# A decoder layer with a mixture of experts: the last layer norm moved into the last two experts

## The chip, the cores and the metric

One NeuronCore of one Trainium2 chip runs the kernel. The metric is device microseconds (us) of one execution; 1935.22 us is the median of three runs of the kernel before.

## The reference, cut to what matters

The last part of the layer, on N = 4096 tokens (rows) of D = 512 values, with 32 experts and 8 experts per token:

```
x      = layernorm(layernorm(x + self_attention) + cross_attention)
logits = x @ gate.T;  topw, topi = top_k(softmax(logits), 8);  topw /= topw.sum()
for each expert e: h = silu(rows_e @ gate_e) * (rows_e @ up_e);  out_e = h @ down_e
ffn    = sum over a token's 8 experts of topw * out_e
out    = layernorm(x + ffn)
```

An expert holds up to 512 rows (CAP). A slot that no token fills points at one of 512 spare rows behind the 4096.

## The kernel before, in words

The layer norms, the attentions and the routing come first (batches of 256 tokens, software-pipelined by hand-written lists of steps) and are not touched. After them `acc_rows` in HBM, 4096 + 512 rows of fp32, holds the input of the expert layer, and each expert adds its rows into it.

**The expert loop.** Experts 0 to 31 (NX = 32) run one after another, with two sets of buffers, k = 0 for even and k = 1 for odd ones. Each engine has its own instruction queue in program order, and semaphores tie them together:

- TensorE: `up_gate` (L1127 on): three column blocks f, for each the gate and the up matmuls (24 matmuls of 128x512 a block, fp32 emulated by three fp16 products, all recorded at L679). Then `down` (L1145): 36 matmuls into four banks `ps_y[c]`, f outermost. The last expert has `down_last` (L1161) in place of it: it waits for all of h and goes c outermost, so that `ps_y[0]` is ready first.
- ScalarE: splits the high part of the next expert's weights (L1289), takes the silu of each gate block (L1545), then writes `y[:, k, c] = ps_y[c] * cur_w` (L1554), four ACTIVATEs of 128x512.
- VectorE: splits the low part of the next expert's weights (L1579), and for each f makes h in three instructions (L2211 product, L2216 cast, L2218 remainder).
- GpSimd: copies the expert's routing weights (L2471), gathers the rows of expert e + 2 by four indirect DMAs of 128 rows (L2477), waits until all scatters of the expert before have landed (`st_y`), copies the row numbers (`column_out`, L2464) and scatters y with four indirect DMAs that add in memory (`scatter`, L2490, `compute_op=ALU.add`).
- SyncE (SP): loads the weights of expert e + 2 into `stage[:, place]`, waits for the gathered rows and transposes them (`turn_tokens`, L629) for TensorE.

**The last stage.** SP waits for `st_y` = 32 * 64, that is until every scatter has landed (L657). It then loads `acc_rows` in 8 groups of 512 rows (GROUPS = 8, GT = 4 tiles of 128 rows, 1 MB each, L666) into `rows3`, which lies over the weights' arena. For each group VectorE makes four `bn_stats` (L2235), four `bn_aggr` (L2238) and two small instructions (L2240, L2241); GpSimd raises the variance to the power -1/2 and makes the shift (L2527, L2529); ScalarE scales four tiles in place (L1569); SP stores the group to `out` (L669) and waits at the end for all eight stores.

Rows are laid out `(t p)`, so each partition's four rows of a group lie apart in HBM and one contiguous piece has 2 KB:

```python
            def group_rows(ap, g):
                return ap[bass.ds(g * GT * P, GT * P), :].rearrange("(t p) n -> p t n", p=P)
```

## Time and profile before

| | us |
|---|---|
| median of 3 runs | 1935.22 (1933.79 to 1937.46) |
| the profiled execution, its own time | 1940.54 |
| its span, first to last record | 1938.7 |
| TensorE busy | 1818.9 (94% of the span) |
| VectorE, ScalarE, GpSimd busy | 1163.9, 978.0, 1218.6 |
| from the last matmul's end to the end of the span | 52.7 (from 1886.0) |

All times of day in this document are microseconds from the start of the span. TensorE's time fills the span up to 1886.0, where the last expert's matmuls end; behind them stand the last scatters, the loads, the norm and the stores.

### The profile page before, as it was taken

The page shows a single profiled execution, that of the slowest core. Times are in us where ns is not written, and L with a number is a line of the kernel's source. Part 1 is how long each engine was busy: PE and PEld are TensorE (multiplying, and loading weights), DVE is VectorE, ACT ScalarE, POOL GpSimd, SP SyncE. Part 2 cuts the span into 40 slices and gives each one's busy share as a digit, 9 for nine tenths or more (in the row PEclk, how much of TensorE's full clock was granted, in tenths as well). Part 3 has the DMA queues.
Part 4 walks back from the last instruction along what each step waited for, and adds up shares of the span by engine and source line. Part 5 has one row for each costly group of instructions (what it writes and reads, how often), then busy time and mean ns, then how long its engine had stood idle before and what let it go on. Part 6 is the DMA issues. An engine that isn't in the chain of part 4 may idle for free.

```text
span 1938.7 us, 43204 instructions
## 1 busy us (share of the span) xinstructions
PE 1818.9 (94%) x15510; PEld 1082.8 (56%) x15510; DVE 1163.9 (60%) x2145; ACT 978.0 (50%) x1969; POOL 1218.6 (63%) x992
## 2 busy tenths in 40 slices
PE   7999999999999999999996769999999999999980
PEld 4776676667767776777763424444444444444430
DVE  5546778777877787778776734444444444444434
ACT  6766666676666665766572313333333333333314
POOL 3766766776677767776775046666666656566632
PEclk8999999999999999999998779999999999999995
DMA  8775776566566656576647389999999999999949
GB/s 236 144 134 115 138 137 143 117 144 151 126 131 130 155 131 132 120 158 136 133 100 174 106 220 233 234 243 233 239 231 245 241 248 241 246 231 235 199 58 352
DMA packets 619374, 345.17 MB, mean 178 GB/s; under 512 B 519344, under 2 KB 541872, under 8 KB 619312
## 3 DMA queue, kind: packets, MB, share of 16 engines
q1 hardware_dynamic: 590368, 274.09, 59.1%
q0 software_dynamic: 28944, 70.27, 17.5%
q8 instruction: 36, 0.59, 0.1%
q14 instruction: 26, 0.21, 0.0%
HBM read 158.67 MB, written 60.29 MB: 113 GB/s over the span
## 4 chain that ended last, share of the span: by engine, by line
PE 88%; DMA 3%; ACT 3%; DVE 3%; issue 2%; POOL 1%; SPq 1%; ACTq 0%; DVEq 0%; POOLq 0%
PE bank L679 62%; PE bank L1145 12%; PE bank L745 5%; PE bank L717 5%; ACT arena_wo L1569 1%; PE bank L873 1%; PE bank L689 1%; PE bank L780 1%; DMA arena_a<-stage 1%; DMA arena_p<-x_rows,cur_from 0%; PE bank L817 0%; DVE s_max L1609 0%; DMA stage<-wkT 0%; ACT qk L1202 0%; DMA arena_wo<-acc_rows 0%
## 5 line engine op out<-in xcount | busy, mean ns | idle before, releaser
L679 PE MATMUL bank<-arena_x,arena_wo 128*128 128x256 f16 (+1 forms) x4224 | 611.3, 303 | 8.2 <-ACT qk L1202 5.3
L679 PEld LDWEIGHTS bank<-arena_x,arena_wo 128*128 128x128 f16 x4224 | 409.1, 98 | 196.8 <-issue 10.7
L2490 POOL DMA_INDIRECT acc_rows<-arena_wo,cur_to x128 | 274.5, 2144 | 240.7 <-ACT arena_wo L1554 211.2
L2273 POOL TENSOR_TENSOR arena_p<-arena_p 128x512 f16<-128x512 f32 x256 | 329.3, 1308 | 109.8 <-ACT arena_p L1221 109.8
L1579 DVE SCALAR_TENSOR_TENSOR arena_wo<-stage,arena_wo 128x3072 f16<-128x3072 f32 (+2 forms) x70 | 174.2, 2490 | 290.2 <-ACT arena_wo L1289 280.1
L679 PE MATMUL bank<-arena_v,arena_wo 128*128 128x512 f16 x1152 | 253.9, 382 | 18.0 <-DMA arena_v<-arena_p 18.0
L1145 PE MATMUL bank<-arena_wo 128*128 128x512 f16 x1116 | 245.9, 379 | 0.0
L2268 POOL TENSOR_TENSOR qk<-qk 128x512 f16<-128x512 f32 x128 | 161.6, 1263 | 116.7 <-ACT qk L1202 116.6
L1212 ACT ACTIVATE arena_p<-bank,s_neg 128x256 f32<-128x256 f32 x512 | 203.4, 504 | 15.9 <-DVE s_neg L1612 13.4
L1554 ACT ACTIVATE arena_wo<-bank,cur_w 128x512 f32<-128x512 f32 x128 | 79.8, 686 | 256.8 <-PE bank L1145 246.9
L1200 ACT ACTIVATE qk<-bank,bqkv 128x256 f32<-128x256 f32 x256 | 123.2, 481 | 153.3 <-PE bank L679 152.8
L679 PEld LDWEIGHTS bank<-arena_v,arena_wo 128*128 128x128 f16 x1152 | 113.2, 98 | 156.2 <-issue 22.0
L1545 ACT ACTIVATE arena_a<-bank 128x512 f32<-128x512 f32 x96 | 57.0, 594 | 271.8 <-PE bank L679 262.7
L1609 DVE TENSOR_REDUCE s_max<-bank 128x2 f32<-128x512 f32 x256 | 164.2, 683 | 40.6 <-PE bank L717 40.4
L1145 PEld LDWEIGHTS bank<-arena_wo 128*128 128x128 f16 x1116 | 109.2, 98 | 131.7
L679 PE MATMUL bank<-arena_wo,arena_x 128*128 128x512 f16 x768 | 178.2, 382 | 0.0
L1221 ACT ACTIVATE arena_p<-arena_p 128x512 f16<-128x512 f32 x256 | 152.1, 668 | 43.4 <-issue 39.8
L679 PE MATMUL bank<-arena_wo,arena_a 128*128 128x512 f16 x768 | 171.0, 379 | 1.1 <-DVE arena_r L1646 0.8
L2477 POOL DMA_INDIRECT arena_p<-x_rows,cur_from x124 | 129.5, 1044 | 53.3 <-issue 27.1
L2211 DVE SCALAR_TENSOR_TENSOR arena_a<-bank,arena_a 128x512 f32<-128x512 f32 x96 | 66.0, 688 | 139.7 <-PE bank L679 139.6
L1289 ACT ACTIVATE arena_wo<-stage 128x3072 f16<-128x3072 f32 (+1 forms) x62 | 131.2, 2118 | 0.5 <-DMA stage<-wdnT 0.5
L1202 ACT ACTIVATE qk<-bank,bqkv 128x256 f16<-128x256 f32 x256 | 123.7, 483 | 0.0
(183 smaller groups left out, 2310.1 us busy)
## 6 DMA issues: line engine op xcount, KB each, us to landing
stage<-wguT SPq DMA_DIRECT2D x31, 1536.0 KB
stage<-wdnT SPq DMA_DIRECT2D x31, 768.0 KB
arena_x<-xT SPq DMA_DIRECT2D x16, 512.0 KB, 4.2
arena_r<-x_rows SPq DMA_DIRECT2D x16, 512.0 KB, 5.2
stage<-ctxT SPq DMA_DIRECT2D x16, 512.0 KB, 4.4
x_rows<-arena_r SPq DMA_DIRECT2D x16, 512.0 KB, 3.0
acc_rows<-arena_r SPq DMA_DIRECT2D x16, 512.0 KB, 3.3
arena_wo<-acc_rows SPq DMA_DIRECT2D x8, 1024.0 KB, 10.8
```

The source lines that it names most:

```text
L679: mm = pe.matmul(out_ap, lhs(a, i), rhs(c, i), start=(n == 0 and i == 0), stop=(n == 2 and i == chunks - 1))
L1145: mm = pe.matmul(ps_y[c][:, :], hT[:, a, f, c * P:(c + 1) * P], ew_dn[:, k, w, f, :], start=(f == 0 and n == 0), stop=(f == FC - 1 and n = ...
L1202: ins = nc.scalar.activation(qk[:, j % 2, 0, at], ps_qk[:, at], ACT.Identity, bias=bqkv[:, w, j:j + 1], scale=1.0 / W_SCALE)
L1212: ins = nc.scalar.activation(probs[:, j % 2, h, t, :], ps_s[j % 2][h][:, t * S:(t + 1) * S], ACT.Exp, bias=s_neg[:, j % 2, n:n + 1], scale ...
L1221: nc.scalar.activation(halves[:, j % 2, h, 0, :], probs[:, j % 2, h].rearrange("p t k -> p (t k)"), ACT.Copy).then_inc(p_hi, 1)
L1289: nc.scalar.activation(ew[:, k, 0, part], stage[:, place, part], ACT.Copy, scale=W_SCALE).then_inc(ew_hi, 1)
L1579: return vec.scalar_tensor_tensor(out=dst, in0=src, scalar=scale, in1=hi, op0=ALU.mult, op1=ALU.subtract)
L1609: vec.tensor_reduce(s_max[:, j % 2, 2 * h:2 * h + 2], ps_s[j % 2][h][:, :].rearrange("p (t k) -> p t k", t=TT), AX.X, ALU.max).then_inc(s_ ...
L2268: gp.tensor_tensor(qk[:, j % 2, 1, :], qk32[:, j % 2, :], qk[:, j % 2, 0, :], ALU.subtract).then_inc(qk_lo, 1)
L2273: gp.tensor_tensor(halves[:, j % 2, h, 1, :], probs[:, j % 2, h].rearrange("p t k -> p (t k)"), halves[:, j % 2, h, 0, :], ALU.subtract).t ...
L2477: gp.indirect_dma_start(xg[:, k, c, :], None, x2_rows, bass.IndirectOffsetOnAxis(ap=cur_from[:, k, c:c + 1], axis=0)).then_inc(ld_xg[k], 16)
L2490: gp.indirect_dma_start(acc_rows, bass.IndirectOffsetOnAxis(ap=cur_to[:, k, c:c + 1], axis=0), y[:, k, c, :], None, compute_op=ALU.add).th ...
```

## The change

The last stage is started before the last two experts (30 and 31) have added their rows.

- Once the scatters of expert 29 have landed, SP loads the 8 groups of `acc_rows`, each into a buffer that is free by then: `stage`, `arena_r`, `arena_v` and the even weights' buffer. All eight are normalised and stored to `out`; for tokens of experts 30 and 31 these rows are still incomplete. The layout is now `(p t)`: a partition's four rows are neighbours in HBM, one piece of 8 KB.
- The rows of experts 30 and 31 are finished apart. GpSimd gathers their present sums (`gather_old`), VectorE adds `ps_y * cur_w` to them (`add_rows`, in place of ScalarE's L1554), writes the result to y, and normalises y as a ninth and tenth set (`late`, sets 6 and 9 in order). ScalarE's result goes back into the gathered buffer.
- Expert 30's sums are put back into `acc_rows` (`put_rows`, plain indirect writes) after all groups are loaded, since expert 31 may share tokens with it, and `gather_old` of expert 31 waits for that.
- When all eight stores have landed, the finished rows are written over them in `out` by row number, first expert 30's, and when those have landed expert 31's (`put_late`). `out` gets 512 spare rows, which the host cuts off.
- TensorE's `down_last` is gone; expert 31 uses `down`.
- The order in which the steps stand on VectorE, ScalarE, GpSimd and SP is written out by hand. On GpSimd `scales(0)` to `scales(4)` stand ahead of `put_rows`, `scales(5)` to `scales(9)` behind `gather_old` of expert 31; on VectorE both last groups stand ahead of `add_rows` of expert 31.
- The statistics' small buffers move to `x1T` and have 10 sets.

```diff
# SP
-            sp.wait_ge(st_y, NX * 64)
-            sp.wait_ge(y_done, NX * CC)
...
-            for g in range(GROUPS):
-                if g >= HALF:
-                    sp.wait_ge(ld_acc[g % HALF], 16)
-                sp.dma_start(rows3[:, g], group_rows(acc_rows, g)).then_inc(ld_acc[g % HALF], 16)
-            for g in range(GROUPS):
-                sp.wait_ge(out_done, (g + 1) * GT)
-                sp.dma_start(group_rows(out, g), rows3[:, g]).then_inc(st_out, 16)
+                return ap[bass.ds(g * GT * P, GT * P), :].rearrange("(p t) n -> p t n", p=P)
+            sp.wait_ge(st_y, (NX - LATE) * 64)
+            sp.wait_ge(ew_lo_gu, NX - 1)
+            sp.wait_ge(ew_lo_dn, NX - 1)
+            load_group(0)
+            load_group(1)
+            load_group(2)
+            sp.wait_ge(ew_lo_gu, NX)
+            sp.wait_ge(ew_lo_dn, NX)
+            load_group(3)
+            load_group(4)
+            sp.wait_ge(u_mm, (NX - 1) * FC)
+            load_group(5)
+            store_group(0)
+            sp.wait_ge(y_mm, (NX - 1) * CC)
+            load_group(6)
+            load_group(7)
+            for g in range(1, GROUPS):
+                store_group(g)
             sp.wait_ge(st_out, GROUPS * 16)
+            sp.wait_ge(st_late, LATE * 64)
# TensorE
-            up_gate(NX - 1, 1, NX // 2 * 64)
-            down_last(NX - 1, 1)
+            expert(NX - 1, 1, NX // 2 * 64)
# ScalarE
+            def scaled(n, dst, rows, done):
+                act.wait_ge(ln3_rstd, 2 * (n + 1))
+                for t in range(GT):
+                    nc.scalar.activation(dst[:, t, :], rows[:, t, :], ACT.Identity, bias=shift3[:, n, t:t + 1],
+                                         scale=rstd3[:, n, t:t + 1]).then_inc(done, 1)
...
+            gate_out(NX - 2, 0, 2)
+            group(0, 0)
+            gate_out(NX - 1, 1, 0)
+            group(1, 1)
+            gate_out(NX - 1, 1, 1)
+            group(2, 2)
+            gate_out(NX - 1, 1, 2)
+            group(3, 3)
+            group(4, 4)
+            group(5, 5)
+            late(6, 0)
+            group(7, 6)
+            group(8, 7)
+            late(9, 1)
# VectorE
+            def add_rows(e, k):
+                for c in range(CC):
+                    dve.wait_ge(y_mm, count(e, CC, c + 1))
+                    if c == 0:
+                        dve.wait_ge(cur_done, count(e, 2, 2))
+                        dve.wait_ge(ld_old[k], CC * 16)
+                    vec.scalar_tensor_tensor(out=y[:, k, c, :], in0=ps_y[c][:, :], scalar=cur_w[:, k, c:c + 1],
+                                             in1=old[k][:, c, :], op0=ALU.mult, op1=ALU.add).then_inc(y_done, 1)
...
+            up_out(NX - 2, 0, 2)
+            group(0, 0)
+            group(1, 1)
+            add_rows(NX - 2, 0)
+            group(2, 2)
+            up_out(NX - 1, 1, 0)
+            group(3, 3)
+            up_out(NX - 1, 1, 1)
+            group(4, 4)
+            up_out(NX - 1, 1, 2)
+            group(5, 5)
+            late(6, NX - 2, 0)
+            group(7, 6)
+            group(8, 7)
+            add_rows(NX - 1, 1)
+            late(9, NX - 1, 1)
# GpSimd
+            def put_rows(e, k):
+                for c in range(CC):
+                    wait_apart(pool, y_done, count(e, CC, c + 1), s_const, N_CONST)
+                    gp.indirect_dma_start(acc_rows, bass.IndirectOffsetOnAxis(ap=cur_to[:, k, c:c + 1], axis=0),
+                                          y[:, k, c, :], None).then_inc(st_y, 16)
...
+            pool.wait_ge(xg_turned[0], NX // 2 * 64)
+            weights_out(NX - 2, 0)
+            pool.wait_ge(cur_done, count(NX - 2, 2, 2))
+            pool.wait_ge(st_y, (NX - 2) * 64)
+            column_out(NX - 1, 1)
+            gather_old(NX - 2, 0)
+            pool.wait_ge(xg_turned[1], NX // 2 * 64)
+            weights_out(NX - 1, 1)
+            scales(0)
...
+            scales(4)
             for g in range(GROUPS):
+                pool.wait_ge(ld_acc[g], 16)
+            put_rows(NX - 2, 0)
+            pool.wait_ge(cur_done, count(NX - 1, 2, 2))
+            gather_old(NX - 1, 1)
+            for n in range(5, SETS):
+                scales(n)
+            pool.wait_ge(st_out, GROUPS * 16)
+            put_late(0, 0)
+            pool.wait_ge(st_late, CC * 16)
+            put_late(1, 1)
```

`up_out`, `gate_out`, `rows_out`, `spread`, `scales` are the old loops' bodies with names; `gather_old(e, k)` waits for `st_y >= e * 64` and issues four indirect reads of `acc_rows` into `old[k]`; `put_late(n, k)` issues four indirect writes from `old[k]` into `out`.

## Rows read from the trace of the kernel before

**Rows 1.** The profile's page: its first line, and the last chain's shares by engine.

```profile
span 1938.7 us, 43204 instructions
...
PE 88%; DMA 3%; ACT 3%; DVE 3%; issue 2%; POOL 1%; SPq 1%; ACTq 0%; DVEq 0%; POOLq 0%
```

**Rows 2.** The chain of work that ended last, in order of time: start, us, what.

```profile
1860.49 15.55 PE bank L679 x72
...
1880.23 0.70 ACT arena_wo L1554
...
1887.49 5.48 DMA acc_rows<-arena_wo,cur_to
...
1892.99 5.65 DMA arena_wo<-acc_rows
```

**Rows 3.** Timeline, GpSimd, expert 29's scatter, then the last expert's: start, us, engine, what.

```profile
1836.90 1.63 POOL L2490 DMA_INDIRECT acc_rows<-arena_wo,cur_to  x1 [5.53 <-ACT arena_wo L1554]
...
1840.72 4.67 POOL L2490 DMA_INDIRECT acc_rows<-arena_wo,cur_to  x1 [0.31 <-issue]
...
1850.70 0.19 POOL L2464 COPY cur_to<-idx_to 128x4 int32<-128x4 int32 x1 [3.13 <-DMA acc_rows<-arena_wo,cur_to]
...
1881.69 1.58 POOL L2490 DMA_INDIRECT acc_rows<-arena_wo,cur_to  x1 [14.00 <-ACT arena_wo L1554]
```

**Rows 4.** Timeline, the last loads and stores on SP's queue, and ScalarE's 32 scalings.

```profile
1892.99 14.56 SPq L666 DMA_DIRECT2D arena_wo<-acc_rows  x8
...
1903.13 23.37 ACT L1569 ACTIVATE arena_wo<-arena_wo,arena_r 128x512 f32<-128x512 f32 x32 [16.39 <-POOL arena_r L2529]
...
1907.59 20.22 SPq L669 DMA_DIRECT2D out<-arena_wo  x8
```

**Rows 5.** Busy time by stretch: PE, PEld, DVE, ACT, POOL, granted clock, DMA share, GB/s.

```profile
1855.00:1860.00 5.00, 5.00 (x25) 2.29 (x24) 0.00 (x0) 1.41 (x3) 0.00 (x0) 1.00 0.00 0
...
1865.00:1870.00 5.00, 5.00 (x25) 2.25 (x23) 1.81 (x3) 0.60 (x1) 2.39 (x3) 1.00 0.99 129
...
1928.00:1933.00 5.00, 0.00 (x0) 0.00 (x0) 0.00 (x0) 0.00 (x0) 0.00 (x0) 0.50 1.05 409
```

**Rows 6.** Timeline, VectorE's first two groups of the last stage and GpSimd's scales between.

```profile
1898.66 2.47 DVE L2235 BATCH_NORM_STATS2 arena_r<-arena_wo 128x6 f32<-128x512 f32 x4 [20.71 <-DMA arena_wo<-acc_rows]
...
1901.52 0.16 DVE L2241 TENSOR_SCALAR arena_r<-arena_r 128x4 f32<-128x4 f32 x1
1901.60 2.46 DVE L2235 BATCH_NORM_STATS2 arena_r<-arena_wo 128x6 f32<-128x512 f32 x4
...
1902.90 0.20 POOL L2529 TENSOR_TENSOR arena_r<-arena_r 128x4 f32<-128x4 f32 x1
```

**Rows 7.** Timeline, VectorE: h of expert 31's first block, and a weight split of expert 30.

```profile
1840.59 3.36 DVE L1579 SCALAR_TENSOR_TENSOR arena_wo<-stage,arena_wo 128x3072 f16<-128x3072 f32 x1 [9.26 <-ACT arena_wo L1289]
...
1865.71 0.69 DVE L2211 SCALAR_TENSOR_TENSOR arena_a<-bank,arena_a 128x512 f32<-128x512 f32 x1 [11.07 <-PE bank L679]
...
1866.97 0.69 DVE L2218 TENSOR_TENSOR arena_wo<-arena_a,arena_wo 128x512 f16<-128x512 f32 x1
```

**Rows 8.** Timeline, GpSimd: the last two gathers' issues, and SP's transposes that wait for them.

```profile
1828.66 0.96 POOL L2477 DMA_INDIRECT arena_p<-x_rows,cur_from  x1 [0.30 <-issue]
...
1829.92 0.96 POOL L2477 DMA_INDIRECT arena_p<-x_rows,cur_from  x1 [0.30 <-issue]
...
1833.80 5.36 SPq L629 DMA_TRANSPOSE arena_x<-arena_p  x4
```

**Rows 9.** Timeline, GpSimd: two scatter issues of expert 30, nothing beside them.

```profile
1863.77 1.56 POOL L2490 DMA_INDIRECT acc_rows<-arena_wo,cur_to  x1 [0.30 <-issue]
1865.64 1.56 POOL L2490 DMA_INDIRECT acc_rows<-arena_wo,cur_to  x1 [0.30 <-issue]
```

**Rows 10.** DMA issues: out<-in, queue, count, KB each, median us from issue to landing.

```profile
x_rows<-arena_r SPq DMA_DIRECT2D x16, 512.0 KB, 3.0
...
out<-arena_wo SPq DMA_DIRECT2D x8, 1024.0 KB, 12.9
```

169 lines of the change are left out of this document (99 added, 70 removed).

## The prediction

> **What bounds the kernel now.** I read the page first: TensorE holds 88% of the chain that ended last [rows 1], so up to the last expert only TensorE's work sets the time, and the change takes none of that away. The chain in order of time shows what follows. The last expert's 72 gate and up matmuls run from 1860.49 to 1876.04, ScalarE's first `ps_y` is written by 1880.93, the last scatter starts at 1887.49 and lands 5.48 later, and SP's first load starts at 1892.99 and takes 5.65 [rows 2]. From there VectorE begins a group every 2.94 us (1898.66, 1901.60) [rows 6], ScalarE takes 23.37 / 8 = 2.92 us a group, and SP issues the last store by 1907.59 + 20.22 = 1927.8 [rows 4]. The DMA engines still move 409 GB/s at a share of 1.05 after that [rows 5], and the span ends at 1938.7 [rows 1]. So behind the last matmul (1886.0) stand 52.7 us, bound by the transfers at their end: 16.8 MB in 44 us. The stretches before show the room: no bytes at all from 1855 to 1860, and 129 GB/s at a share of 0.99 while expert 30's adding scatters run [rows 5]. The granted clock is 1.00, TensorE's upper level of 2.4 GHz, in these two stretches [rows 5]; what follows the matmuls doesn't use TensorE.
>
> **What the change removes.** The whole tail from 1889 on: the wait for the last adding scatters, eight loads and eight stores. They move to 1850.7, the time at which GpSimd saw expert 29's scatters landed [rows 3]. The last two experts' adding scatters (eight issues) and ScalarE's eight L1554 go too. What comes back is a chain of dependent transfers. I follow the path that ends last.
>
> **Start to `scales(4)`.** SP waits for `st_y` of expert 29 alone; both weight conditions are met before, by 1847.5 at the latest, since expert 31's splits stand directly ahead in VectorE's order. The loads start at 1850.7. The first takes 5.65 [rows 2]; it now shares the engines with `gather_old` of expert 30. I add 0.7, the time of its first 128 rows (0.26 MB at 409 GB/s [rows 5]); the bounds are 0 and 2.6, its whole 1.05 MB. Group 0 is there at 1857.0. From here VectorE has work without a gap: five `spread` at 2.94 = 14.7 [rows 6], `add_rows` with four products like L2211 at 0.69 = 2.8, and two times h at 1866.97 + 0.69 - 1865.71 = 1.95, so 3.9 [rows 7]. Sum 21.4, so group 4's statistics end at 1878.4. Nothing else on the way is late: the third block of expert 31 needs the h product of the first, at 1869.2, and starts at 1860.49 + 2/3 x 15.55 = 1870.9 [rows 2]; `down` needs the last h at 1880.4 for its third part, which starts at 1876.04 + 5.3 = 1881.3. TensorE then ends near 1884, 2 us earlier than before, because f is outermost again; that is off the path. The loads must bring group 4 by 1875.5: 5.2 MB plus 1.05 MB gathered in 23 us after the first 2, which needs 276 GB/s. `scales(4)` takes 1902.90 + 0.20 - 1901.68 = 1.4 [rows 6]: 1879.8.
>
> **The round trip through `acc_rows`.** `put_rows` waits for all eight loads. Groups 6 and 7 are issued behind store 0, near 1864.5, and land by some 1873, so that wait costs nothing; if the loads fell behind, `put_rows` would be the next thing late. A batch of four indirect DMAs starts 0.76 after what it waits for (1880.93 to 1881.69 [rows 2, 3]). What a plain indirect write costs, the trace does not show. Below it stands the gather, from issue to issue 1.26 and 0.96 for the last, landing 2.92 after it (1830.88 to 1833.80) [rows 8]: a batch of 0.76 + 3 x 1.26 + 0.96 = 5.5, with landing 8.4. Above it stands the adding scatter, issues 1.87 apart [rows 9], landing 1892.97 - 1887.49 = 5.48 after the last issue began [rows 2]: 0.76 + 5.6 + 5.5 = 11.8. I take the gather: what the scatter has beyond it is the addition, which also shows in 129 GB/s at full share against 409 for plain stores [rows 5], and the new writes have no addition. Stores of group 3 and 4 run beside `put_rows`; I add 0.4. So 1879.8 + 8.4 + 0.4 = 1888.6. `gather_old` of expert 31 issues for 5.5, to 1894.1, and only then comes `scales(5)`: 1895.5. This is where the gain is lost again: ScalarE has stood still since group 4 (1882.7), though group 5's statistics are there at 1883.3.
>
> **ScalarE to the end.** Four sets (group 5, late 6, groups 6 and 7) at 2.92 [rows 4] end at 1907.2. VectorE gets expert 31's old rows at 1897.0, ends late 9 at 1902.7, and its scaling ends at 1910.1, hidden behind the stores and `put_late(0)`. Store 7 has an almost empty queue ahead of it: half a MB lands in 3.0 [rows 10], and another half at 409 GB/s takes 1.3; I take 4.5. The bounds are 4.3 and the first load's 5.65 [rows 2]; the 12.9 of the stores now [rows 10] is their queue. All stores are down at 1911.7. `put_late(0)` and `put_late(1)` are each a batch with landing, one after the other: 8.4 + 8.4, so 1928.5. That is 10.2 less than 1938.7. Statistics buffers, the longer `out` and the 8 KB pieces I cost at nothing: the first is only an address, the second is cut off on the host, the third is hidden behind VectorE's 2.94 a group.
>
> **The Trainium skill, DMA: Bandwidth & Descriptors, section Anatomy of one DMA,** gives 2.0 us and bytes over 436 GB/s for a DMA issued from GpSimd. That would be 4.4 for a MB, where the first load shows 5.65 [rows 2], so the trace disagrees there, and 2.6 for the last 128 rows of a batch, where the trace has 2.92. By the page the sum would be 1.25 + 3 x 0.3 + 0.1 = 2.3 lower; the sum above goes by the rows.
>
> **Size of it.** The profiled execution's own time is 1940.54, 1.8 above its span, and 5.3 above the median of the runs, 1935.22. I take the 10.2 off the median: **1925.0 us**. About 0.2% (3.9 us) is what a measurement of this kernel can tell from no change.
>
> **Rivals.**
> 1. *A plain indirect write costs what an adding scatter costs.* For: 1.56 against 0.96 may come from the direction and not the addition; no row parts the two. Against: the rates above. Three such batches are on the path: 3 x (11.8 - 8.4) = 10.2, so 1935.2, no change. With only the issues at the scatter's pitch (3 x 2.4) it is 1932.3. Chance 0.19.
> 2. *A batch is slower than either, and the kernel is slower.* Expert 29's scatter took from 1836.90 to 1850.70 with one issue of 4.67 in it [rows 3]; with 0.76 that is 14.6 a batch, and three give 1925.0 + 18.6 = 1943.6. The place is the same three batches; it decides from (10.2 + 3.9) / 3 = 4.7 more a batch, that is from 13.1. For: nothing can hide them, each waits for the one before. Against: the long issue started 0.13 us after a VectorE split of 3.36 us [rows 3, 7], and VectorE is idle during both `put_late`. Chance 0.07.
> 3. *VectorE's statistics hold GpSimd's issues.* `put_rows` would start when VectorE has finished h, groups 5, 6, 7 and late 6: 1878.4 + 1.95 + 4 x 2.94 = 1892.1 instead of 1880.6, so 1936.5, no change. Against: L2529 takes 0.20 amid statistics [rows 6], as short as an undisturbed copy, 0.19 [rows 3]. Chance 0.04. The Trainium skill, SBUF — State Buffer, section Who interferes with whom, lets a VectorE instruction contend with GpSimd only with two SBUF inputs or in a two-port mode; by it the statistics hold nothing, the h steps could, and those end at 1880.4, just ahead of `put_rows`.
> 4. *The loads are slow.* At half the rate, 204 GB/s, group 4 comes at 1883.6 instead of 1875.5, and all behind it moves by 8.1: 1933.1, no change. For: 8 KB pieces in a new order, three queues at once. Against: 409 GB/s with 2 KB pieces [rows 5]. Chance 0.04.
>
> **The numbers.** The forecast has 0.66. Its own bounds: down 0.7 (no gather beside the load), 0.4 (no store beside `put_rows`), 0.2 (store), and 0.6 for each landing if it took a plain store's 1.7 and 0.6 for the rows, so 1921.9; up 1.9, 1.2 and a part of the batch's range, so 1930. With the spread of the runs, 1920 is the low end. The high end takes in the first rival in full, and the fourth: 1935.5; the second and most of the third are left out. Faster by over 0.2% is the forecast and a small part of the fourth, 0.68; within 0.2% are the first, third and the rest, 0.25; slower is the second, 0.07.
>
> **What would show it.** Right: loads issued at 1850.7 and VectorE gapless from 1857 to 1880; `put_rows` issues 1.26 apart from 1880.6; ScalarE idle from 1882.7 to 1895.5 before group 5; the last `out` store landing near 1911.7 with its landing under 6; then two batches of 8.4 and nothing else until 1928.5. Wrong: issues 1.87 apart or landings over 5 (first rival, second if a batch passes 13); a first `put_rows` issue at 1892 (third); VectorE waiting for `ld_acc` after group 0 (fourth). If ScalarE starts group 5 much before 1895, the order on GpSimd isn't the bound that I make it.

## The result, and the profile after

The changed kernel takes 1928.15 us (median of 7 runs, 1927.25 to 1930.16), the kernel before, run beside it, 1936.86 (7 runs, 1933.79 to 1939.74). The ratio is 0.9959 [0.9947, 0.997], so 8.7 us faster, outside the 0.2% that a measurement can tell from nothing. The forecast was 1925.0, so 3.1 too low, and inside the range.

The profiled execution has a time of its own of 1929.34 us, 1.7 above its span. First the page, its first line and the last chain's shares by engine, which answer to [rows 1]:

```profile
span 1927.6 us, 43260 instructions
...
PE 86%; DVE 3%; DMA 3%; issue 3%; POOL 2%; ACT 2%; SPq 1%; POOLq 0%; DVEq 0%; ACTq 0%
```

TensorE's share falls by two points, although nothing was taken from its expert loop: the chain now leaves TensorE earlier and goes through VectorE, the transfers and GpSimd. The reader should see that a share says where the chain runs, not what was gained.

A span isn't a clean measure here. Expert 31's first matmul starts at 1860.33 in the timeline of the kernel before and at 1856.66 after the change, and over the profiled executions below at anything from 1851.94 to 1874.86, though the code ahead of the change's stretch is the same. So I use the **tail**, from that matmul to the end of the span: 1938.7 - 1860.33 = 78.4 before, 1927.6 - 1856.66 = 70.9 after. That is 7.5 less (the medians say 8.7). The prediction's tail was 1928.5 - 1860.33 = 68.2, so what has to be explained is 2.8 us.

The timeline of the changed kernel's tail (start, us, engine, line, operation, and in brackets the idle time of the engine before it and what ended it), which answers to [rows 2 to 4, 6 to 9]:

```profile
1847.25 0.82 SPq L671 DMA_DIRECT2D stage<-acc_rows  x2
...
1852.10 2.47 DVE L2279 BATCH_NORM_STATS2 x1T<-stage 128x6 f32<-128x512 f32 x4 [1.13 <-DMA stage<-acc_rows]
...
1856.66 10.52 PE L705 MATMUL bank<-arena_x,arena_wo 128*128 128x512 f16 x48
...
1861.76 2.73 DVE L2272 SCALAR_TENSOR_TENSOR arena_wo<-bank,cur_w,arena_r 128x512 f32<-128x512 f32 x4 [3.47 <-DMA arena_r<-acc_rows,cur_to]
...
1868.06 5.36 PE L705 MATMUL bank<-arena_x,arena_wo 128*128 128x512 f16 x24 [0.88 <-DVE arena_a L2249]
...
1877.00 1.01 POOL L2597 TENSOR_TENSOR x1T<-x1T,neg_half 128x4 f32<-128x4 f32 x1 [2.96 <-DVE x1T L2285]
...
1878.01 0.69 DVE L2256 TENSOR_TENSOR arena_wo<-arena_a,arena_wo 128x512 f16<-128x512 f32 x1
1878.09 0.67 POOL L2599 TENSOR_TENSOR x1T<-x1T 128x4 f32<-128x4 f32 x1
...
1879.16 1.07 POOL L2592 DMA_INDIRECT acc_rows<-arena_wo,cur_to  x1 [0.40 <-issue]
...
1883.07 0.96 POOL L2592 DMA_INDIRECT acc_rows<-arena_wo,cur_to  x1 [0.30 <-issue]
...
1889.71 1.00 POOL L2586 DMA_INDIRECT arena_p<-acc_rows,cur_to  x1 [5.67 <-DMA acc_rows<-arena_wo,cur_to]
...
1895.87 2.93 ACT L1580 ACTIVATE arena_v<-arena_v,x1T 128x512 f32<-128x512 f32 x4 [14.14 <-POOL x1T L2599]
...
1904.46 3.15 SPq L675 DMA_DIRECT2D out<-arena_wo  x2
...
1911.40 1.06 POOL L2604 DMA_INDIRECT out<-arena_r,cur_to  x1 [6.91 <-DMA out<-arena_wo]
...
1918.28 0.96 POOL L2604 DMA_INDIRECT out<-arena_p,cur_to  x1 [2.01 <-DMA out<-arena_r,cur_to]
...
1922.08 0.96 POOL L2604 DMA_INDIRECT out<-arena_p,cur_to  x1 [0.30 <-issue]
```

Three brackets stand out. VectorE waited 3.47 us for expert 30's gathered rows, a wait that the sum didn't have. ScalarE stood still for 14.14 us until `scales(5)`, which the sum did have (12.8). GpSimd waited 5.67 us for `put_rows` to land, where the sum had 2.92 + 0.4 for the landing and 0.76 for the start of what follows it, so 4.1. The last issue ends at 1922.08 + 0.96 = 1923.04, and the span ends only 4.6 later, at 1927.6.

By stretch (PE, PEld, DVE, ACT, POOL busy with counts, granted clock, DMA share, GB/s), which answers to [rows 5]:

```profile
1850.00:1886.00 36.00, 30.48 (x140) 13.28 (x138) 30.71 (x88) 16.15 (x23) 14.15 (x18) 1.00 1.01 410
1886.00:1927.60 41.60, 0.00 (x0) 0.00 (x0) 10.07 (x32) 14.20 (x20) 17.58 (x22) 0.51 0.44 165
1925.00:1927.60 2.60, 0.00 (x0) 0.00 (x0) 0.00 (x0) 0.00 (x0) 0.00 (x0) 0.50 0.00 0
```

The empty stretch of before [rows 5] is now full: the DMA engines run at a share of 1.01 and 410 GB/s for 36 us. Behind it they are at 0.44, and every engine mostly waits for another. So the tail has two halves, one bound by transfers and one by a row of dependent steps.

The page's DMA issues (queue, count, KB each where it is plain, median us from issue to landing) for the changed kernel, beside [rows 10], and two rows of SP's waits (us in total, times, longest):

```profile
arena_r<-acc_rows,cur_to POOLq DMA_INDIRECT x4, 8.4
...
arena_p<-acc_rows,cur_to POOLq DMA_INDIRECT x4, 3.6
...
out<-arena_r,cur_to POOLq DMA_INDIRECT x4, 2.7
...
out<-arena_wo SPq DMA_DIRECT2D x2, 1024.0 KB, 3.9
```

```profile
SPq L696 <- DMA out<-arena_p,cur_to: 17.2, 1, 17.2
...
SPq L79 <- PEq L79: 2.5, 1, 2.5
```

A gather of the same size lands in 8.4 us beside the loads and in 3.6 when the engines are half idle (share 0.45 between 1889 and 1897). SP's wait puts the last landing at 1904.46 + 3.15 + 17.2 = 1924.8.

### The profile page after: what moved, and what is told of

Same layout as the page of the kernel before. It is cut to its first block, busy times and chain, and to the rows that moved or that the text cites. A ratio compares the mean times of both kernels' runs of the same rounds, so it can differ in the third digit from the quotient of the medians.

```text
span 1927.6 us, 43260 instructions
## 1 busy us (share of the span) xinstructions
PE 1815.8 (94%) x15510; PEld 1080.1 (56%) x15510; DVE 1172.6 (61%) x2173; ACT 976.7 (51%) x1969; POOL 1215.3 (63%) x1008
## 4 chain that ended last, share of the span: by engine, by line
PE 86%; DVE 3%; DMA 3%; issue 3%; POOL 2%; ACT 2%; SPq 1%; POOLq 0%; DVEq 0%; ACTq 0%
PE bank L705 61%; PE bank L1171 12%; PE bank L771 5%; PE bank L743 5%; PE bank L899 1%; PE bank L715 1%; PE bank L806 1%; DMA acc_rows<-arena_wo,cur_to 1%; DVE x1T L2279 0%; DMA arena_r<-acc_rows,cur_to 0%; DMA arena_a<-stage 0%; POOL arena_p L2562 0%; DMA stage<-wvT 0%; POOL acc_rows L2568 0%; PE bank L843 0%
## 5 line engine op out<-in xcount | busy, mean ns | idle before, releaser
L2568 POOL DMA_INDIRECT acc_rows<-arena_wo,cur_to x120 | 236.2, 1969 | 227.4 <-ACT arena_wo L1565 199.9
L1171 PE MATMUL bank<-arena_wo 128*128 128x512 f16 x1152 | 254.1, 379 | 0.2 <-DVE arena_wo L2256 0.2
L1565 ACT ACTIVATE arena_wo<-bank,cur_w 128x512 f32<-128x512 f32 x120 | 74.5, 685 | 239.1 <-PE bank L1171 239.1
L2555 POOL DMA_INDIRECT arena_p<-x_rows,cur_from x124 | 124.6, 1005 | 53.3 <-issue 27.7
```

Source lines behind the costliest of these rows:

```text
L1171: mm = pe.matmul(ps_y[c][:, :], hT[:, a, f, c * P:(c + 1) * P], ew_dn[:, k, w, f, :], start=(f == 0 and n == 0), stop=(f == FC - 1 and n = ...
L2555: gp.indirect_dma_start(xg[:, k, c, :], None, x2_rows, bass.IndirectOffsetOnAxis(ap=cur_from[:, k, c:c + 1], axis=0)).then_inc(ld_xg[k], 16)
L2568: gp.indirect_dma_start(acc_rows, bass.IndirectOffsetOnAxis(ap=cur_to[:, k, c:c + 1], axis=0), y[:, k, c, :], None, compute_op=ALU.add).th ...
```

## The experiments

Two theories stood at the start. **Mine:** VectorE's order and its 3.47 us wait carry through to the end, and after it GpSimd's order (scales behind the gather) holds ScalarE. **The rival:** VectorE is covered, and what sets `put_rows`' landing is the 36 us of full DMA engines. Beside them stood the two dear-write rivals of the prediction, and a theory of the end: a fixed close of GpSimd behind its last DMA issue. Each edit is made to the changed kernel unless the text says otherwise. All of them in one table (medians in us, ratio to the kernel before in the same runs; a line without a ratio is a single execution, and span, first matmul and tail are always those of the one profiled execution):

| kernel | median | ratio | span | first matmul | tail |
|---|---|---|---|---|---|
| changed kernel | 1928.15 | 0.9959 [0.9947, 0.997] | 1927.6 | 1856.66 | 70.9 |
| scales 5 to 7 ahead of the gather | 1926.66 | 0.9943 [0.9925, 0.9961] | 1925.8 | 1858.80 | 67.0 |
| group 2 ahead of the sum | 1929.20 | 0.9959 [0.9946, 0.9973] | 1927.7 | 1856.83 | 70.9 |
| late writes with an addition | 1940.26 | | 1938.5 | 1858.54 | 80.0 |
| 2 KB pieces | 1932.17 | 0.9982 [0.9963, 1.0002] | 1939.1 | 1866.78 | 72.3 |
| kernel before, 8 KB pieces | 1936.17 | 1.0 [0.9981, 1.0019] | 1930.6 | 1853.52 | 77.1 |
| stores held | 1926.19 | 0.9941 [0.9915, 0.9967] | 1920.2 | 1852.38 | 67.8 |
| `put_late(0)` ahead of the last scales | 1921.03 | 0.991 [0.9884, 0.9936] | 1921.7 | 1858.11 | 63.6 |
| GpSimd waits for the last landing | 1938.49 | | 1936.8 | 1863.90 | 72.9 |
| new order, stores held | 1921.57 | 0.9921 [0.9908, 0.9935] | 1915.3 | 1852.63 | 62.7 |
| new order, stores free | 1922.65 | 0.9924 [0.9911, 0.9938] | 1918.7 | 1854.47 | 64.2 |
| loads held for the gather | 1927.97 | | 1926.2 | 1851.94 | 74.3 |
| new order, scales 6 ahead too | 1921.18 | 0.9915 [0.99, 0.993] | 1937.1 | 1874.86 | 62.2 |

How well a tail repeats shows in two kernels whose edit comes late. The one in which GpSimd waits at its very end is the changed kernel up to its last issue, and that issue ends 66.4 us after the first matmul in both (1930.26 - 1863.90, 1923.04 - 1856.66). With additions, the first late write starts 55.0 us after it, against 54.7. So 0.3 us of a tail say nothing, and a microsecond does.

The medians move less than the tails. Against the changed kernel they gain 1.5 us (scales ahead), 2.0 (stores held), 7.1 (`put_late(0)` ahead) and 6.6 (new order, stores held), where the tails gain 3.9, 3.1, 7.3 and 8.2. The intervals of the first two overlap with the changed kernel's, so their gain is shown by the tails and not by the time of the whole kernel.

### Scales ahead of the second gather

```diff
             put_rows(NX - 2, 0)
+            scales(5)
+            scales(6)
+            scales(7)
             pool.wait_ge(cur_done, count(NX - 1, 2, 2))
             gather_old(NX - 1, 1)
-            for n in range(5, SETS):
-                scales(n)
+            scales(8)
+            scales(9)
```

> Edit on the changed kernel: GpSimd makes scales 5, 6 and 7 between put_rows and gather_old of expert 31 instead of behind it. Theory: the end hangs on GpSimd's order; ScalarE idles 14.1 us (1881.7 to 1895.9) although group 5's statistics end at 1881.6. Then ScalarE starts group 5 by 1886, does late 6 and group 6, waits for scales(8) behind the gather (about 1896), stores are down near 1903 instead of 1911, and the kernel is 7 to 9 us faster than the changed one, about 1920. Rival (the end hangs on the transfers, the stores or the gathered rows): under 2 us faster, because expert 31's rows still come at 1897.

Measured: tail 67.0, so 3.9 less, and not the 7 to 9 expected. The timeline of this kernel (columns as above):

```profile
1887.70 2.93 ACT L1580 ACTIVATE arena_v<-arena_v,x1T 128x512 f32<-128x512 f32 x4 [3.70 <-POOL x1T L2599]
...
1901.84 2.73 DVE L2272 SCALAR_TENSOR_TENSOR arena_wo<-bank,cur_w,arena_p 128x512 f32<-128x512 f32 x4 [9.15 <-DMA arena_p<-acc_rows,cur_to]
...
1907.70 1.01 POOL L2597 TENSOR_TENSOR x1T<-x1T,neg_half 128x4 f32<-128x4 f32 x1 [9.42 <-DVE x1T L2285]
...
1909.60 1.06 POOL L2604 DMA_INDIRECT out<-arena_r,cur_to  x1 [0.61 <-issue]
```

ScalarE's wait before group 5 fell from 14.14 to 3.70, so GpSimd's order was the bound of that step. But `put_late(0)` now starts 0.61 behind `scales(9)` and not behind the stores: what is late next is GpSimd's queue itself. `scales(9)` waits 9.42 us for VectorE's last statistics, and with it everything queued behind it. The gather also got slower: its last issue ended at 1896.92 and VectorE had the rows at 1901.84, 4.9 later, where it was 2.9 in the changed kernel. The stores came earlier and now run beside it, which is the likely reason. Both took from the gain.

### Group 2 ahead of expert 30's sum

```diff
             group(1, 1)
-            add_rows(NX - 2, 0)
             group(2, 2)
+            add_rows(NX - 2, 0)
             up_out(NX - 1, 1, 0)
```

> Edit on the changed kernel: VectorE does group 2 ahead of add_rows of expert 30, where it waited 3.47 us for the gathered rows. Theory (gather_old of expert 30 is late beside the loads, and the VectorE path to scales(4) carries to the end): the wait goes, group 4's statistics end 2.5 to 3.5 us earlier, TensorE's stall of 0.88 us goes, and the end comes 2.5 to 3.5 us earlier, about 1925. Rival (the end is not tied to VectorE here but to the loads of groups 6 and 7, which put_rows waits for): statistics earlier, but the first put_rows issue moves by under 1 us and the end too.

Measured: tail 70.9, no change. The timeline:

```profile
1856.83 15.70 PE L705 MATMUL bank<-arena_x,arena_wo 128*128 128x512 f16 x72
...
1877.76 1.07 POOL L2592 DMA_INDIRECT acc_rows<-arena_wo,cur_to  x1 [1.85 <-DMA arena_wo<-acc_rows]
...
1889.82 1.00 POOL L2586 DMA_INDIRECT arena_p<-acc_rows,cur_to  x1 [7.19 <-DMA acc_rows<-arena_wo,cur_to]
```

The local effect is all there: VectorE's 3.47 us wait is gone, TensorE runs 72 matmuls without its stall of 0.88, and `put_rows` is issued 20.9 us after the first matmul and not 22.5, so 1.6 earlier, where the rival had under 1. And nothing of it arrives. `put_rows` waits for the last loads (1.85), as the rival had it, then 7.19 for its landing, where it was 5.67; the gather starts 33.0 us after the first matmul, as in the changed kernel (1889.71 - 1856.66 = 33.05). My theory of VectorE's path falls here, and with it the step of the prediction that followed VectorE.

### The stores held back while the rows are put

```diff
-            for g in range(1, GROUPS):
+            store_group(1)
+            store_group(2)
+            sp.wait_ge(st_y, (NX - 1) * 64)
+            for g in range(3, GROUPS):
                 store_group(g)
```

> Edit on the changed kernel: SP holds stores 3 and later until expert 30's rows have landed in acc_rows (st_y). e2 showed that put_rows lands at the same time although it was issued 1.4 us earlier. Theory (the DMA engines, full from 1850 to 1886, set when put_rows lands, and stores 3 and 4 stand in them beside it): the last put_rows lands 2 to 3 us after its issue instead of 5.2, gather_old and all behind it come 2 to 3 us earlier, and the tail from expert 31's first matmul is 68 to 69 us instead of 70.9. Rival (the landing of an indirect write to HBM just takes 5 us when other writes are under way, or the loads set it): put_rows lands as late as before, the tail is the same or longer by the stores' delay.

Measured: tail 67.8, 3.1 less, though a wait was only added. The timeline:

```profile
1878.84 0.96 POOL L2595 DMA_INDIRECT acc_rows<-arena_wo,cur_to  x1 [0.30 <-issue]
1882.32 1.00 POOL L2589 DMA_INDIRECT arena_p<-acc_rows,cur_to  x1 [2.52 <-DMA acc_rows<-arena_wo,cur_to]
```

With two stores (2.1 MB) out of the way the rows are seen down 2.52 us after their last issue's end and not 5.67. So most of that wait was other transfers in the DMA engines, and not a property of an indirect write. The held stores then stand beside the gather, which takes 6.5 us from issue to landing and not 3.6. Nothing of that reaches the end here, as ScalarE and the stores have idle time until `scales(5)`.

### Both late writes with an addition

This kernel leaves the output changed: the two last writes add the finished rows to the stored ones.

```diff
                     gp.indirect_dma_start(out, bass.IndirectOffsetOnAxis(ap=cur_to[:, k, c:c + 1], axis=0),
-                                          old[k][:, c, :], None).then_inc(st_late, 16)
+                                          old[k][:, c, :], None, compute_op=ALU.add).then_inc(st_late, 16)
```

> Edit on the changed kernel: both put_late batches add in memory (compute_op=ALU.add), so the finished rows are added to what the stores wrote instead of replacing it. It prices an indirect write with and without the addition in one place with idle transfers. Theory (the addition makes the scatter dear): issues 1.87 apart instead of 1.27, landing of the last over 3.5 us after its issue began instead of 2.7, each batch 10 to 11 us instead of 6.9, the end 6 to 8 us later, about 1935. Rival (it is the direction, as rival 1 of the prediction had it): no difference, which is already excluded for the issues if they stay 1.27 apart here.

Measured: tail 80.0, 9.0 more, a little over the 6 to 8 expected. The timeline:

```profile
1913.54 1.66 POOL L2604 DMA_INDIRECT out<-arena_r,cur_to  x1 [6.96 <-DMA out<-arena_wo]
...
1919.22 1.54 POOL L2604 DMA_INDIRECT out<-arena_r,cur_to  x1 [0.30 <-issue]
1925.06 1.54 POOL L2604 DMA_INDIRECT out<-arena_p,cur_to  x1 [4.30 <-DMA out<-arena_r,cur_to]
```

A batch now takes 1925.06 - 1913.54 = 11.5 us where the plain one takes 1918.28 - 1911.40 = 6.9. The issues are 1.86 apart where they were 1.27, and the wait for the landing is 4.30 where it was 2.01. Rows, tiles and direction are the same, so the addition alone costs 4.6 us a batch. The first rival asked whether direction or addition makes a scatter dear, and this answers it; the prediction's price for the addition, 11.8 - 8.4 = 3.4 a batch, was too low.

### The piece size, in the changed kernel and in the kernel before

In the changed kernel, back to 2 KB pieces:

```diff
             def group_rows(ap, g):
-                return ap[bass.ds(g * GT * P, GT * P), :].rearrange("(p t) n -> p t n", p=P)
+                return ap[bass.ds(g * GT * P, GT * P), :].rearrange("(t p) n -> p t n", p=P)
```

> Edit on the changed kernel: the groups' rows are laid out (t p) again, pieces of 2 KB instead of 8 KB, loads and stores. Theory (piece size matters little between 400 and 429 GB/s): the first load lands in 4.5 to 5.7 us instead of 4.5, the six loads together with the gather come up to 2 us later, and the end by 0 to 2 us. Rival (the large pieces hold the gathered rows up, since the engines change between queues by whole pieces): the gather of expert 30 lands 2 to 4 us earlier than now, VectorE's wait for it shrinks from 3.5 us, and the end comes 1 to 3 us earlier.

In the kernel before, 8 KB pieces alone:

```diff
             def group_rows(ap, g):
-                return ap[bass.ds(g * GT * P, GT * P), :].rearrange("(t p) n -> p t n", p=P)
+                return ap[bass.ds(g * GT * P, GT * P), :].rearrange("(p t) n -> p t n", p=P)
```

> Edit on the kernel before: only the group's layout, (p t) instead of (t p), pieces of 8 KB; nothing else of the change. Its tail is bound by transfers (409 GB/s). Theory (the layout is a small part of the gain of its own): the rate rises to the 420 to 429 GB/s of the changed kernel's stretch, 16.8 MB take 1 to 2 us less, the kernel is 1 to 2.5 us faster than before. Rival (the pieces carry no gain; the gain is all from the overlap): within 0.5 us.

Measured: with 2 KB pieces the changed kernel's tail is 72.3, 1.4 more; with 8 KB pieces the tail of the kernel before is 77.1, 1.3 less, and its ratio of 1.0 [0.9981, 1.0019] can't show that. First a line of the timeline of the changed kernel with 2 KB pieces, then one of the busy time by stretch of the kernel before with 8 KB pieces:

```profile
1868.34 2.47 DVE L2279 BATCH_NORM_STATS2 x1T<-stage 128x6 f32<-128x512 f32 x4 [2.39 <-DMA stage<-acc_rows]
```

```profile
1920.00:1925.00 5.00, 0.00 (x0) 0.00 (x0) 0.00 (x0) 0.00 (x0) 0.00 (x0) 0.50 1.00 424
```

With 2 KB pieces VectorE waits 2.39 us for group 1's load, where with 8 KB ones the same step followed the last one's end by 0.14. In the kernel before the rate rises from 409 GB/s [rows 5] to 424. The piece size is worth a little over a microsecond in either kernel, by one tail each. The rival, that large pieces hold the gathered rows up, holds in a small part: with 2 KB pieces the gather lands in 7.1 us and not 8.4, where 2 to 4 less were asked, and VectorE doesn't wait for it, since it now waits for the loads ahead of it. The tail explains 1.4 of the 4.0 us between the medians (1932.17, 1928.15). The rest stands ahead of it, over code that is the same: the profiled execution (1940.86) reached expert 31 10.1 us later than the changed kernel's (1866.78 against 1856.66), and why isn't known.

### `put_late(0)` ahead of the last scales

```diff
             put_rows(NX - 2, 0)
+            scales(5)
+            scales(6)
+            scales(7)
             pool.wait_ge(cur_done, count(NX - 1, 2, 2))
             gather_old(NX - 1, 1)
-            for n in range(5, SETS):
-                scales(n)
+            scales(8)
             pool.wait_ge(st_out, GROUPS * 16)
             put_late(0, 0)
+            scales(9)
```

> Edit on the changed kernel: e1's, and put_late of expert 30 ahead of scales(9). In e1 put_late(0) stood behind scales(9), whose statistics came at 1907.6 because the gathered rows of expert 31 landed 5.9 us after their last issue, beside two stores. Theory: put_late(0) starts when the last store is down, near 1905 on e1's clock instead of 1909.6, and the tail from expert 31's first matmul is 62 to 63.5 us, against 67.0 in e1 and 70.9 in the changed kernel. Rival (put_late(1) then waits for late 9's scaling instead): the tail is 65 or more, since scales(9) stands behind put_late(0)'s issues.

Measured: 1921.03 us, tail 63.6, 3.4 less than with the scales moved alone, and near the 62 to 63.5 expected. The timeline:

```profile
1904.35 1.05 POOL L2604 DMA_INDIRECT out<-arena_r,cur_to  x1 [7.11 <-DMA out<-arena_wo]
...
1912.25 1.03 POOL L2604 DMA_INDIRECT out<-arena_p,cur_to  x1 [1.66 <-ACT arena_p L1580]
```

The first late batch waits for the stores again, and `scales(9)` with ScalarE's last set fit almost behind it: only 1.66 us show before `put_late(1)`. Four sets of scales, each in another place of GpSimd's queue, are worth 7.3 us of tail, about what the whole change was (7.5); by the medians it is 7.1 against 8.7.

### A wait for the last landing on GpSimd

```diff
             put_late(1, 1)
+            pool.wait_ge(st_late, LATE * CC * 16)
```

> Edit on the changed kernel: GpSimd's program ends with a wait for the landing of the last put_late instead of with its issue. In the changed kernel the last landing is seen by SP at 1924.8 and the span ends at 1927.6, 4.5 us after GpSimd's last issue ended. Theory (closing GpSimd takes a fixed 3 to 4.5 us behind its last instruction, here overlapping the landing): the end moves out by 1 to 2 us behind the landing. Rival (GpSimd's close waits for its transfers, and then takes 2.5 us): the end stays 2.8 us behind the landing.

Measured: tail 72.9, 2.0 more. The timeline's last line, and the page's wait that answers:

```profile
1929.30 0.96 POOL L2604 DMA_INDIRECT out<-arena_p,cur_to  x1 [0.30 <-issue]
```

```profile
SPq L79 <- PEq L79: 4.5, 1, 4.5
```

In the changed kernel that wait is 2.5. The span ends 1936.8 - 1930.26 = 6.5 us after the last issue and not 4.6, and 4.8 after the landing (1932.0) and not 2.8. If SP's wait for the landing set the end, another engine's wait for the same landing would cost nothing. It costs 2.0, about the time from the last issue's end to the landing (1924.8 - 1923.04 = 1.8). So a part of GpSimd's close comes after whatever it does last, and isn't covered by the landing.

Is the close a fixed time behind the last issue, as the theory has it? In three kernels it looks so: `put_late(1)` ends its last issue at 1923.04, 1917.11 and 1915.63, and the spans end at 1927.6, 1921.7 (`put_late(0)` ahead) and 1920.2 (stores held), each 4.6 later. But the landing comes 1.8 after the issue's end in all three, so they can't tell the issue from the landing. The kernel with additions can, since its landing is later. A line of its timeline and two rows of SP's waits:

```profile
1930.61 1.55 POOL L2604 DMA_INDIRECT out<-arena_p,cur_to  x1 [0.30 <-issue]
```

```profile
SPq L696 <- DMA out<-arena_p,cur_to: 26.2, 1, 26.2
...
SPq L79 <- PEq L79: 2.3, 1, 2.3
```

SP's last store issue ends there at 1909.74, so the last landing is seen at 1935.9, and the span ends at 1938.5: 6.3 after the last issue's end (1932.16), but 2.6 after the landing. A fixed 4.6 behind the issue fails here, and a fixed time behind the landing fails where GpSimd waits. What fits all of them is a close with some 2 us that can run beside the landing and some 2.6 behind it. That is an estimate from these kernels and wasn't tested further.

### A new order of all three queues, with the stores held and free

VectorE takes group 2 ahead of the sum. SP loads groups 6 and 7 ahead of the first store. GpSimd puts the rows ahead of `scales(4)`. Expert 30's late rows become set 8, behind all groups.

```diff
             load_group(5)
-            store_group(0)
             sp.wait_ge(y_mm, (NX - 1) * CC)
             load_group(6)
             load_group(7)
-            for g in range(1, GROUPS):
+            store_group(0)
+            store_group(1)
+            store_group(2)
+            sp.wait_ge(st_y, (NX - 1) * 64)
+            for g in range(3, GROUPS):
                 store_group(g)
...
-            late(6, 0)
-            group(7, 6)
-            group(8, 7)
+            group(6, 6)
+            group(7, 7)
+            late(8, 0)
...
             scales(3)
-            scales(4)
...
             put_rows(NX - 2, 0)
+            scales(4)
+            scales(5)
             pool.wait_ge(cur_done, count(NX - 1, 2, 2))
             gather_old(NX - 1, 1)
-            for n in range(5, SETS):
-                scales(n)
+            scales(6)
+            scales(7)
+            scales(8)
             pool.wait_ge(st_out, GROUPS * 16)
             put_late(0, 0)
+            scales(9)
```

> All that the runs so far point to, in one kernel. On the changed kernel: group 2 ahead of add_rows of expert 30 (e2); loads 6 and 7 ahead of store 0; put_rows ahead of scales(4), so that the loads alone set its start; scales 4 and 5 between put_rows and gather_old, put_late(0) ahead of scales(9) (e7); expert 30's set after the groups, so that the last store starts a set earlier; stores 3 and later held until put_rows has landed (e6). Theory (transfers set the first half, GpSimd's and ScalarE's order the second): put_rows issues by 16 us after expert 31's first matmul instead of 22.5, and the tail from that matmul is 56 to 60 us, against 70.9 in the changed kernel and 63.6 in e7; in time some 0.9 to 1.3% below the kernel before. Rival (the stores that are held pile up and the DMA engines bound the end): the tail is over 61 us, and the last store lands over 8 us after its issue.

The same without the holding:

```diff
-            store_group(1)
-            store_group(2)
-            sp.wait_ge(st_y, (NX - 1) * 64)
-            for g in range(3, GROUPS):
+            for g in range(1, GROUPS):
                 store_group(g)
```

> e9 without holding the stores. Theory as e6 has it: stores 0 to 3 stand in the DMA engines beside put_rows, it lands over 4 us after its last issue instead of 2 to 3, gather_old of expert 31 comes later by as much, and the tail is 1 to 3 us longer than e9's. Rival: once put_rows is issued behind the last load, the pile of held stores costs as much as it gives, and e10 is as fast as e9 or faster.

Measured: tails 62.7 held and 64.2 free. Holding is worth 1.5 of tail, as expected; in the medians (1921.57, 1922.65) it doesn't show, as their intervals overlap. The 56 to 60 for the held one was missed. Its rival had a tail over 61, which came, and a last store that lands over 8 us after its issue, which didn't (4.7 after the issue's end). The timeline of the held one, then one line of the free one:

```profile
1871.14 1.07 POOL L2595 DMA_INDIRECT acc_rows<-arena_wo,cur_to  x1 [3.91 <-DMA arena_wo<-acc_rows]
...
1881.05 1.03 POOL L2589 DMA_INDIRECT arena_p<-acc_rows,cur_to  x1 [2.44 <-DMA acc_rows<-arena_wo,cur_to]
...
1892.96 2.73 DVE L2275 SCALAR_TENSOR_TENSOR arena_wo<-bank,cur_w,arena_p 128x512 f32<-128x512 f32 x4 [9.36 <-DMA arena_p<-acc_rows,cur_to]
...
1898.03 1.06 POOL L2607 DMA_INDIRECT out<-arena_r,cur_to  x1 [8.36 <-DMA out<-arena_wo]
```

```profile
1885.35 1.03 POOL L2586 DMA_INDIRECT arena_p<-acc_rows,cur_to  x1 [5.65 <-DMA acc_rows<-arena_wo,cur_to]
```

`put_rows` is issued 18.5 us after the first matmul (22.5 in the changed kernel) and is bound by the last load, which it waits for 3.91 us. The held stores then run beside the gather: its last issue ends at 1885.85, and VectorE has the rows 7.1 later, where that was 2.9 in the changed kernel (1894.48 to 1897.34) and 2.8 in the free one. Time moved from the landing of `put_rows` to that of the gather. The stores still end the chain (8.36).

### The loads held for the first gather

```diff
             load_group(0)
             load_group(1)
+            sp.wait_ge(ld_old[0], CC * 16)
             load_group(2)
```

> Edit on the changed kernel: SP holds load 2 and later until expert 30's old rows have been gathered (ld_old). Theory (the gathered rows are late because the loads' 8 KB pieces take most of each engine's time beside their 2 KB rows): the gather lands 3 to 5 us after its issue instead of 8.4 to 9.7, VectorE does not wait for it, TensorE's 0.88 us stall goes; but the DMA engines stand idle for a time, so put_rows lands no earlier and the tail is 70.9 or up to 3 us longer. Rival (a gather beside any load takes 8 us whatever is queued): its landing stays over 7 us.

Measured: tail 74.3, 3.4 more, a little over the 0 to 3 expected. The timeline:

```profile
1876.21 1.07 POOL L2593 DMA_INDIRECT acc_rows<-arena_wo,cur_to  x1 [4.73 <-DMA arena_wo<-acc_rows]
...
1888.33 1.00 POOL L2587 DMA_INDIRECT arena_p<-acc_rows,cur_to  x1 [7.24 <-DMA acc_rows<-arena_wo,cur_to]
```

VectorE's wait for the gather is gone, as with group 2 ahead, and TensorE's stall with it. But the third load was issued 9.9 us after the first (1852.38 and 1842.48), where it had been 0.86 (1848.11 and 1847.25), and every byte behind it came later: `put_rows` waited 4.73 for the loads, then 7.24 for its landing. The gather itself still took 6.1 us with two loads ahead of it, where the theory had 3 to 5 and the rival over 7. Shortening a wait on VectorE by idling the DMA engines costs what it idles.

### One more set of scales ahead

The held order, and `scales(6)` ahead of the second gather too:

```diff
             scales(5)
+            scales(6)
             pool.wait_ge(cur_done, count(NX - 1, 2, 2))
             gather_old(NX - 1, 1)
-            scales(6)
             scales(7)
```

> Edit on e9: scales(6) ahead of gather_old of expert 31, whose four issues held ScalarE for 4.07 us in e9 with group 6's statistics ready. Theory (ScalarE's start on the last two groups sets the last store and so put_late(0)): ScalarE's wait there goes, put_late(0) starts 1.5 to 2 us earlier behind expert 31's first matmul (45.4 us in e9), and the tail is 60.5 to 61.5 us instead of 62.7. Rival (the transfers set the last store's landing in e9, since stores 3 to 7 were pushed together): put_late(0) starts within 0.5 us of e9's and the tail stays at 62 to 63.

Measured: tail 62.2, 0.5 less than in the held order, and not the 60.5 to 61.5 of the theory. By stretch, up to the first late write:

```profile
1902.00:1919.80 17.80, 0.00 (x0) 0.00 (x0) 5.87 (x21) 11.20 (x16) 6.31 (x8) 0.50 0.89 353
```

ScalarE's wait in the last groups fell from 4.07 to 2.02, and the last store was issued 2.8 us earlier (37.9 us after the first matmul, 40.7 in the held order). `put_late(0)` came only 0.4 earlier, 45.0 us after it and not 45.4: with the DMA share at 0.89 the store lands later by nearly all of the 2.8. So the rival held: the transfers set the end of the stores again, not ScalarE. What limits the last stores of this order more closely is open.

## Why the prediction was right, and where it was off

The mechanism held: the stage starts under expert 30, the tail becomes a chain of transfers, and most of the loads' time is hidden. `put_rows` started at once behind `scales(4)`, ScalarE waited for `scales(5)` behind the gather, and behind the last store came two batches. The times of day fit closer than they should: group 5 started at 1895.87 (predicted 1895.5), and the last store was seen down at 1911.4 (1911.7). That is luck, since this execution reached expert 31 3.7 us earlier than the one of before. Counted from there, group 5 came 39.2 us later and not 35.2, and the store 54.7 and not 51.4. Against the terms, measured from expert 31's first matmul, the sum comes out as follows.

| step of the sum | predicted | measured | difference |
|---|---|---|---|
| loads' issue, before the first matmul | 9.6 | 9.4 | +0.2 |
| first load to VectorE | 6.35 | 4.85 | -1.5 |
| VectorE, load 0 to group 4's statistics | 21.4 | 24.8 | +3.4 |
| `scales(4)` | 1.4 | 1.8 | +0.4 |
| `put_rows` to the gather's first issue | 9.6 | 10.95 | +1.4 |
| gather's issues, `scales(5)` | 6.1 | 6.2 | 0 |
| ScalarE's four sets to the last store's issue | 11.7 | 11.4 | -0.3 |
| last store to the first late issue | 5.3 | 4.15 | -1.1 |
| first late batch to the next one's start | 8.4 | 6.9 | -1.5 |
| second late batch to its landing | 7.7 | 6.5 | -1.2 |
| from there to the span's end | 0 | 2.8 | +2.8 |

The differences sum to 2.6 of the 2.8 us (the rest is rounding). VectorE's stretch, the landing of `put_rows` and the end cost more than the sum had, by 7.6 together; five cheaper steps gave 5.6 back. So the total is better than its parts, and that too is luck.

- **"From here VectorE has work without a gap."** Wrong. It waited 3.47 us for the old rows of expert 30, since a gather of four times 128 rows issued among six loads lands in 8.4 us from its issue, and not in the 0.96 + 2.92 that the prediction had for one beside nothing [rows 8]. The prediction added 0.7 us for the gather at the load, but nothing for the loads at the gather. TensorE's third block, which it had on time, waited 0.88 us for VectorE behind this; that is off the path.
- **The path itself.** The sum went through VectorE and gave the transfers 276 GB/s of need against 409. The kernel with group 2 ahead shows that VectorE's gap is covered: the engines are full from 1850 to 1886, and what comes earlier only waits longer for its landing. The numbers of these steps (+3.4, +1.4) are the same stretch of full engines seen twice. The step that failed is the one that asked if the loads bring group 4 in time, and didn't ask what eight loads, a gather and the stores leave for `put_rows`. The loads of groups 6 and 7 show it: the sum had them down some 8.5 us after their issue (1864.5 to 1873), and they took 14.7. In the changed kernel that cost nothing, as VectorE was late too; with group 2 ahead `put_rows` waits for them, which the prediction named as the next thing that would be late.
- **`put_rows` "landing 2.92, + 0.4".** Off: 5.67 from the issue's end to the gather's start, where the sum had 4.1 with its 0.76. The stores were the cause, as the held stores show (2.52). The Trainium skill, DMA: Bandwidth & Descriptors, section Anatomy of one DMA, has a fixed time and a rate that make 2.6 us for 128 such rows, an estimate from its figures. The trace agrees where the engines were idle (`put_late`, 2.7 from issue to landing) and not where they were full. The prediction also held the 4.4 us of this fit for 1 MB against SP's first load (5.65) and called that a disagreement; the fit is for a DMA issued from GpSimd, so that row says nothing on it.
- **The span's end.** The prediction ended with the last landing. The trace of before gave no warning, as GpSimd was long done there: SP waits 10.5 us for the last store, sees it down at 1938.3, and the span ends 0.4 later. With GpSimd last, 2.8 us stand behind the landing.
- **Landings taken high.** The late batches landed 2.7 us after the start of their issue and not 0.96 + 2.92; that a row of gathers with SP's transposes behind it [rows 8] stood in for writes is the likely reason, and wasn't tested. The last store landed in 3.9 and not 4.5.

**The rivals.** The first had two signs, issues 1.87 apart or landings over 5. The second one came, as `put_rows` landed 5.87 after its last issue began, but from the stores and not from the write: issues are 1.27 apart, `put_late` is seen down after 2.01, and with the stores held `put_rows` after 2.52. The kernel with additions shows what a scatter's price in the two late batches alone would have made of it (tail 80.0, more than the 78.4 of before). The second rival fell with batches of 6.9 us, and of 10.55 for `put_rows`, below its 13.1. The third fell: `put_rows` was issued at 1879.16 amid VectorE's statistics, each issue as long as elsewhere. The fourth fell by its sign, as VectorE waited for no load after group 0, and the rate was not low (410 GB/s). But it looked in the right place: the full engines were what bound the middle of the tail.

**The range.** It took in the first rival, which was not needed. What a landing costs beside other transfers was in it with 0.4; the wait of 5.67 against the 2.01 of `put_late` says 3.7.

**What is open.** The two late batches go one after the other because both may write the same rows; letting them run side by side would be a race and wasn't tried. The changed kernel gains 8.7 us by the medians and 7.5 by the tails of one execution each; the time up to expert 31 differs between executions by more than that gap, and I can't say which of the two is nearer.

## What to carry to other kernels

When a stage is moved under other work, price each landing at the load that the DMA engines will have then, not at that of the row it comes from, and add up the bytes of the whole stretch before following any engine. On a queue that runs in order, put the step that waits longest last: moving four small steps on GpSimd gained nearly as much as the whole change, and four of these versions are faster than both kernels (1921.03, 1921.18, 1921.57 and 1922.65 us, not distinguishable from each other). Compare such tails from a fixed point in the work, since the stretch before it can vary by more than the effect.

## What the runs showed of the hardware

- **A landing depends on its neighbours.** A gather of four times 128 rows takes 3.6 us from issue to landing with the engines half idle, 6.1 behind two loads and 8.4 among six. A plain indirect write of the same size is waited for 2.01 us after its issue with idle engines, 2.52 with stores held and 5.67 beside stores.
- **An addition costs both ends.** An issue of 1.55 us and not 0.96, 1.86 apart and not 1.27, and 4.6 us more a batch of 512 rows.
- **A program whose last work is on GpSimd ends later behind the last landing.** The span ends 2.8 us behind it where GpSimd ends with the issue of a plain write (4.6 behind that issue), 2.6 with an addition (6.3), and 4.8 where GpSimd waited for the landing first (6.5); 0.4 in the kernel before, where GpSimd was long done.
- **Piece size.** In the kernel before, the last three full stretches of 5 us give 424 to 429 GB/s with 8 KB pieces and 408 to 409 with 2 KB ones. In the changed kernel the 36 us from 6.66 ahead of expert 31's first matmul give 410 and 392.
- **GpSimd held by VectorE.** `scales`' second operation took 0.67 us and not 0.20 when it started 0.08 after VectorE's L2256, and ended 0.06 after it (1878.76, 1878.70). The Trainium skill, SBUF — State Buffer, section Who interferes with whom, has a VectorE instruction with two SBUF inputs contend with a GpSimd one that reads SBUF. L2256 is one, and this row agrees; beside the statistics, with one input, the operation stays at 0.20.
- **The same code varies.** In the last kernel's profiled execution expert 31's first matmul started at 1874.86, 18.2 later than in the changed kernel's. That execution took 1938.86 us, where the other six of its kernel took 1918.36 to 1921.44. Of the 18.2 us, 12.5 are TensorE waiting for transposed rows in the expert loop: between 1140 and 1500 it is busy for 347.5 of 360 us, where the changed kernel has all 360. These are two rows of its waits in that stretch (us in total, times, longest):

```profile
PE bank L708 <- DMA arena_x<-arena_p: 8.0, 2, 4.8
...
PE bank L708 <- DMA arena_v<-arena_p: 4.5, 2, 2.7
```
